# Search operations issued in batches with two buffers, last down features stacked, an end by halves, and gate weights split by halves

## The chip, the cores and the metric

The kernel runs on one core of one Trainium2 chip. The metric is the device time of one execution in microseconds, the median of several runs. The core has five engines with instruction streams of their own: TensorE (PE) for matmuls and transposes, VectorE (DVE), ScalarE (ACT), GpSimd (POOL) and SyncE (SP), which here issues DMAs. Each works its own stream in order, and they meet only in semaphores: an instruction that waits holds back all that stands behind it on its engine.

## The reference, cut to what matters

```python
# x [16, 64, 1024], ctx [16, 1601, 256], w_gate and w_up [2752, 1024], w_down [1024, 2752]
x = x + attention(layernorm(x), ctx, ctx, mask)       # 32 heads of 32 over 8 key heads
s = silu(layernorm(x) @ w_gate.T)                     # 1024 tokens x 2752 features
k = int(0.5 * 2752)
_, idx = top_k(-abs(s), k)                            # the half with the least magnitude ...
s[rows, idx] = 0.0                                    # ... becomes 0, token by token
x = x + (s * (layernorm(x) @ w_up.T)) @ w_down.T
x = x + mixture(layernorm(x))                         # 8 experts of rank 16, the top 2 by a router
```

## The kernel before, in words

All of it is one program, `fast`, in one block (L634). The 1024 tokens are 8 tiles of 128. Its stages, one after the other on TensorE, are attention (to about 594 us of the span), the gate projection, the up projection, the down projection with the mixture worked into its last third, and an end for the last two tiles. Products are made exact enough by splitting each operand in a rounded high part and a low part, and adding three products (high by high, high by low, low by high).

**Gate.** 16 passes (two halves of the tokens by 8 chunks of 352 features) of 4 tiles each make 64 slots q. For each load of weights, SP loads `g_raw`, ACT rounds it to `g_hi` in one copy (`take_weights`, L1718), POOL subtracts to `g_lo` (L1209), and the pass's first tile waits for `g_lo` (`gate`, L1981). ACT takes each slot's result from PSUM (`take_gate`), SP stores it to `s` in DRAM.

**Up.** 42 blocks i (21 chunks of 128 features by two halves of the tokens) of 24 matmuls each (`up`, L2003), into four PSUM banks: up(i) waits until ACT has copied block i - 4 (`u_copied`, L1786). POOL splits the weights (L1217, L1219). SP stores each `u_out` to `u_t`, and ACT's copy i waits for the store of i - 4.

**Search.** Beside the second half of the gate and all of up, DVE finds for each token the threshold that leaves half the features. It works in pairs of tiles, 0 to 3. `guess(p)` waits for the magnitudes of both tiles (`measure` on ACT) and gives the first cut; then come seven rounds (`search`), in which DVE counts one tile's values below the cut (L1392), ACT counts the other's (`compare`, L1746), and small DVE operations (L1399 to L1421) make the next cut. Then for each tile DVE takes the nearest values below the cut (`near`, L1429), the 8 greatest (L1435), picks the threshold, and `keep` (L1462, L1465) clears what is below it in `sx`. SP loads `mag` (three buffers) and `sx` (one buffer) from `s`, and stores the kept tile to `sk`. At which slot or block each `compare`, `measure`, load and store stands in ACT's and SP's programs is written out by hand in tables (`GATE_COUNT_AT`, `UP_COUNT_AT`, `UP_ABS_AT`, `UP_MAG_AT`, `UP_SK_AT`).

**Down.** 66 steps n: three groups of tiles (0 to 2, 3 to 5, 6 and 7) by 22 chunks of features, the last of 64. Each step turns the kept values of the group (`turn`, L2017), multiplies by `t_u` on DVE (L1495), rounds on ACT (`take_high`, L1803), subtracts on DVE (L1504), and adds 6 matmuls of 512 columns per tile to the tile's two banks (`down`, L2033). POOL splits `w_down` in three buffers (L1229, L1233) and starts a step's when the step three before it is done. The turned values come from `t_sk` blocks (two steps each, three buffers) and `t_u` chunks, loaded from ACT's queue; the first are issued at i = 40 of up. At the end the last two steps do tile 6 first, then tile 7.

**End.** For tiles 6 and 7: add to `xin` (`add_in`, L1515), layer norm (L102 to L114), turn and route (L2053, L2063), the two best experts on DVE, an exponential on ACT (L1815), `turn_hw` (L2075), `mix` (L2084), the last addition (L1561) and the store of the tile (L1070).

## Time and profile before

| | us |
|---|---|
| median of 3 runs | 1415.43 (1413.87 to 1415.97) |
| the profiled execution | 1412.86 |
| its span | 1410.9 |
| TensorE busy | 1362.0 (97%) |
| DVE busy | 981.2 (70%) |
| POOL busy | 929.2 (66%) |
| ACT busy | 739.2 (52%) |

TensorE is busy 97% of the span, so that its idle time and the length of its own work are what there is to look at. In the chain of work that ended last it has 77%, DVE 13% and DMAs 4%. The page puts the matmuls of attention (L1896, L1914, L1933), the gate (L1981), up (L2003) and down (L2033) on top. Times in the rows are us from the span's start, durations in us unless marked ns; the letter q behind an engine (SPq) marks its DMA issues.

### The profile page before, as it was taken

What the parts mean: (1) busy time and instruction counts of PE and PEld (TensorE: products, weight loads), DVE (VectorE), ACT (ScalarE), POOL (GpSimd) and SP (SyncE); (2) the same over time, 40 slices, a digit from 0 to 9 for tenths busy, and PEclk for the clock granted to TensorE, in tenths of its full rate; (3) what the DMA queues carried; (4) which work ended last, traced back from release to release, by engine and by line L of the source; (5) the groups of instructions that cost most, each with busy time, mean ns of one, the idle gap of its engine ahead of it and who ended that gap; (6) DMA issues with size and microseconds to landing.
All of it is one profiled execution on the core that took longest, in us unless ns stands there. A gap on an engine that the chain in (4) does not pass through costs nothing.

```text
span 1410.9 us, 30485 instructions
## 1 busy us (share of the span) xinstructions
PE 1362.0 (97%) x12727; PEld 1014.1 (72%) x12727; DVE 981.2 (70%) x1324; ACT 739.2 (52%) x935; POOL 929.2 (66%) x613
## 2 busy tenths in 40 slices
PE   4999999999999999899999999999997999999996
PEld 4555555555555555599999998888886888887874
DVE  6888888888888888870001899989898223255654
ACT  6788888888888888732224625243331111111211
POOL 0899888888888888813443343223233899999881
PEclk9999999999999999999999999999998999999998
DMA  9023323233333330024337348384736876855561
GB/s 357 33 104 102 136 97 114 99 117 104 117 98 121 100 107 18 16 77 169 139 124 299 122 164 276 126 294 126 275 104 244 299 258 189 272 186 181 160 202 45
DMA packets 110016, 217.62 MB, mean 154 GB/s; under 512 B 7200, under 2 KB 82864, under 8 KB 104880
## 3 DMA queue, kind: packets, MB, share of 16 engines
q1 hardware_dynamic: 88928, 192.89, 39.4%
q10 hardware_dynamic: 20944, 22.70, 5.1%
q8 instruction: 103, 1.69, 0.5%
q14 instruction: 41, 0.34, 0.1%
HBM read 173.63 MB, written 41.94 MB: 153 GB/s over the span
## 4 chain that ended last, share of the span: by engine, by line
PE 77%; DVE 13%; DMA 4%; ACT 3%; issue 2%; POOL 0%; DVEq 0%; ACTq 0%; SPq 0%
PE fast_psum L1896 16%; PE fast_psum L2033 16%; PE fast_psum L1914 15%; PE fast_psum L1981 14%; PE fast_psum L1933 6%; DVE fast_below L1392 4%; PE fast_psum L2003 2%; DMA fast_mag<-s 1%; PE fast_psum L1940 1%; PE fast_psum L2017 1%; PE fast_psum L2063 1%; DMA sk<-fast_sx 1%; PE fast_psum L2084 1%; PE fast_psum L1919 1%; DVE fast_near L1429 1%
## 5 line engine op out<-in xcount | busy, mean ns | idle before, releaser
L1322 DVE TENSOR_TENSOR fast_masked<-fast_psum,fast_mask_t 128x1024 f32<-128x1024 f32 (+1 forms) x416 | 488.2, 1218 | 72.0 <-PE fast_psum L1896 70.4
L1178 POOL TENSOR_TENSOR fast_pair<-fast_probs 128x1024 f32<-128x1024 f32 x192 | 457.0, 2383 | 96.1 <-PE fast_psum L1933 47.9
L1659 ACT ACTIVATE fast_probs<-fast_masked 128x1024 f32<-128x1024 f32 (+1 forms) x416 | 437.8, 1058 | 68.0 <-DVE fast_masked L1322 52.8
L1896 PE MATMUL fast_psum<-fast_qT,fast_kraw 32*128 32x256 f32 (+1 forms) x3328 | 245.7, 401 | 6.5 <-issue 3.3
L1914 PE MATMUL fast_psum<-fast_probs,fast_vraw 128*32 128x256 f32 (+1 forms) x3328 | 226.5, 386 | 0.8 <-ACT fast_probs L1659 0.8
L1896 PEld LDWEIGHTS fast_psum<-fast_qT,fast_kraw 32*128 32x128 f32 (+1 forms) x3328 | 152.9, 181 | 92.6 <-DVE fast_masked L1322 54.0
L1233 POOL TENSOR_TENSOR fast_d_lo<-fast_d_raw,fast_d_hi 128x256 fp32r<-128x256 f32 (+1 forms) x264 | 198.2, 781 | 5.3
L1209 POOL TENSOR_TENSOR fast_g_lo<-fast_g_raw,fast_g_hi 128x2816 fp32r<-128x2816 f32 x14 | 87.8, 6274 | 145.5 <-ACT fast_g_hi L1718 123.4
L1981 PE MATMUL fast_psum<-fast_g_hi,fast_z_hi 128*128 128x352 f32 x512 | 166.4, 325 | 1.8 <-POOL fast_g_lo L1209 1.8
L1981 PE MATMUL fast_psum<-fast_g_hi,fast_z_lo 128*128 128x352 f32 x512 | 165.5, 323 | 0.0
L1981 PE MATMUL fast_psum<-fast_g_lo,fast_z_hi 128*128 128x352 f32 x512 | 165.0, 322 | 0.0
L1914 PEld LDWEIGHTS fast_psum<-fast_probs,fast_vraw 128*32 128x32 f32 (+1 forms) x3328 | 87.1, 109 | 107.3 <-ACT fast_probs L1659 46.5
L1803 ACT CAST fast_h_hi<-fast_t_h 128x384 fp32r<-128x384 f32 (+1 forms) x66 | 31.5, 478 | 221.0 <-DVE fast_t_h L1495 206.8
L2003 PE MATMUL fast_psum<-fast_z_hi,fast_u_hi 128*128 128x512 f32 x336 | 130.8, 389 | 0.6 <-ACT fast_res L1709 0.6
L2003 PE MATMUL fast_psum<-fast_z_hi,fast_u_lo 128*128 128x512 f32 x336 | 130.7, 389 | 0.0
L2003 PE MATMUL fast_psum<-fast_z_lo,fast_u_hi 128*128 128x512 f32 x336 | 130.7, 389 | 0.0
L1495 DVE TENSOR_TENSOR fast_t_h<-fast_psum,fast_t_u 128x384 f32<-128x384 f32 (+1 forms) x63 | 32.2, 512 | 138.6 <-PE fast_psum L2017 134.7
L1217 POOL CAST fast_u_hi<-fast_u_raw 128x1024 fp32r<-128x1024 f32 x21 | 22.7, 1082 | 154.0 <-PE fast_psum L2003 90.5
L2033 PE MATMUL fast_psum<-fast_d_hi,fast_h_hi 128*128 128x512 f32 (+1 forms) x352 | 118.8, 419 | 0.7 <-issue 0.7
L1933 PE MATMUL fast_psum<-fast_pair,fast_ones 128*32 128x256 f32 x1536 | 118.1, 379 | 1.3 <-POOL fast_pair L1178 1.3
L2033 PE MATMUL fast_psum<-fast_d_lo,fast_h_hi 128*128 128x512 f32 (+1 forms) x352 | 109.9, 393 | 0.0
L2033 PE MATMUL fast_psum<-fast_d_hi,fast_h_lo 128*128 128x512 f32 (+1 forms) x352 | 109.6, 393 | 0.0
(164 smaller groups left out, 1898.2 us busy)
## 6 DMA issues: line engine op xcount, KB each, us to landing
fast_d_raw<-w_down SPq DMA_DIRECT2D x63, 512.0 KB, 3.7
fast_kraw<-ctx_t SPq DMA_DIRECT2D x32, 800.5 KB, 6.0
fast_vraw<-ctx_nat SPq DMA_DIRECT2D x16, 1536.0 KB
fast_g_raw<-w_gate_up SPq DMA_DIRECT2D x15, 1408.0 KB, 7.3
fast_mag<-s SPq DMA_DIRECT2D x8, 1376.0 KB, 9.8
fast_sx<-s SPq DMA_DIRECT2D x8, 1376.0 KB, 6.8
sk<-fast_sx SPq DMA_DIRECT2D x8, 1376.0 KB, 7.1
fast_u_raw<-w_up_t SPq DMA_DIRECT2D x21, 512.0 KB, 5.4
```

What stands on the lines that cost most here:

```text
L1178: pool.tensor_tensor(pair[:, n % PAIR_BUFS], both[:, :, 0, :], both[:, :, 1, :], ALU.add).then_inc(paired, 1)
L1209: pool.tensor_tensor(g_lo[j][:, :, :], g_raw[raw(n)][:, :, :], g_hi[j][:, :, :].bitcast(F32), ALU.subtract).then_inc(g_lo_done, 1)
L1233: last = pool.tensor_tensor(d_lo[j][0:r, qs], d_raw[j][0:r, qs], d_hi[j][0:r, qs].bitcast(F32), ALU.subtract)
L1322: dve.tensor_tensor(into, of, m, ALU.add).then_inc(mask_added, 1)
L1392: done(dve.tensor_scalar(below[0], mag[t % MAGS], cut[:, r, t:t + 1], None, ALU.is_lt, ALU.add, accum_out=count[:, t:t + 1]))
L1659: act.activation(probs[0:r, g % RING, hp * HALF:(hp + 1) * HALF], masked[0:r, h % SLOTS, :], ACT.Exp).then_inc(exp_done, 1)
L1896: last = pe.matmul(scores[0:r, (2 * g + hp) % SLOTS, h % 2, i * 256:(i + 1) * 256], kraw[b % BUFS][q, u, c * P:c * P + r], qT[q, b, u, :], ...
L1914: last = pe.matmul(o_acc[q, u, 0:256], vraw[b % BUFS][0:r, c, u * P + h * HD:u * P + (h + 1) * HD], probs[0:r, g % RING, (2 * h + i) * 256 ...
L1933: last = pe.matmul(o_acc[h * HD:(h + 1) * HD, u, 256:512], ones[:, :], pair[:, n % PAIR_BUFS, h, :], start=False, stop=final, skip_group_c ...
L1981: last = pe.matmul(bank[GATE_BANKS[q % GBANKS]][:, 0:GJ], zp[:, k, ts], wp[n % 2][:, k, :], start=(k == 0 and a == 0), stop=(k == DK - 1 a ...
L2003: last = pe.matmul(bank[i % 4][:, :], wp[f % 2][:, k, :], zp[:, k, gs], start=(k == 0 and a == 0), stop=(k == DK - 1 and a == 2))
L2033: last = pe.matmul(bank[2 * i + o][:, :], hp[jh][0:r, ts], wp[j][0:r, o * 512:(o + 1) * 512], start=(k == 0 and a == 0), stop=(k == IC - 1 ...
```

## The change

- `take_weights` rounds each gate load in two copies (4 of the 8 contraction chunks each), POOL subtracts in two, and the first tile of a pass waits for the first half at its start and for the second at its fifth chunk. The first load stays as it is.
- `sx` has two buffers and for tile 7 takes one of `mag`; its loads have a table of their own (`UP_SX_AT`), `load_mag` stands ahead of `load_sx` and `store_sk`, and the store of tile 7 stands in up's loop at f = 19.
- The comparisons of pairs 1 to 3 stand in batches of three, two and one in ACT's program, those of pair 1 behind slot 63, those of pair 2 at i = 11, 13, 16, those of pair 3 at i = 23, 25, 28. The number of rounds is the same.
- `load_block` and `load_u` of the first steps are issued at i = 34 of up; `load_block` waits for the `sk` of six tiles.
- For the last 64 features the kept values, and the weights, are loaded twice, to rows 0 to 63 and 64 to 127. POOL rounds all rows into `d_hi` and puts the low part into rows 64 to 127 of `d_hi`. So one matmul of 128 rows makes two of the three products, and one of 64 rows the third.
- Steps 63 to 65 do tile 6 first, then tile 7. In the last step each half of the columns is finished by itself (`half_done`); DVE adds it and takes its `bn_stats`. `add_out` waits for each half of `mix`, and tile 7 is stored in two halves. An exponential on a constant (`first_exp`) stands before the last use of `take_zt`.
- The slab is aligned to 128 bytes, not 512.

The diff, cut; `rows(k)` is replaced by P also in `multiply`, `take_low`, `take_high`, `turn`.

```diff
@@ -770,7 +775,8 @@
         below = [at(f"below{j}", WIDE + 3 * I + I // 2 * j, [I], BF16)[:, :] for j in range(2)]
-        sx = at("sx", WIDE + 4 * I, [I])[:, :]
+        sx_of = [at(f"sx{j}", start, [I])[:, :] for j, start in enumerate((WIDE + 4 * I, THIN + 2 * HT * GJ))]
+        sx = [sx_of[t % 2] for t in range(TILES - 1)] + [mag[(TILES - 3) % MAGS]]
         t_sk = [at(f"t_sk{j}", THIN + 3 * BW * j, [3, BW]) for j in range(2)] + [
@@ -854,6 +861,13 @@
         steps = [0]
+        g_split = lambda n, h=1: 1 if n == 0 else 2 * n + h
+        HELD = DS
+        twice = lambda n: n % IC == UF
+
+        def loads(n, ring, every=IC):
+
+            return sum(2 if m % every == every - 1 else 1 for m in range(n % ring, n + 1, ring))
...
         def u_loads(n):
...
         GATE_COUNT_AT = {42: (0, 0), 44: (0, 1), 45: (0, 2), 46: (0, 3), 48: (0, 4), 49: (0, 5)}
-        UP_ABS_AT = {6: 4, 12: 5, 19: 6, 25: 7}
-        UP_COUNT_AT = {0: (1, 0), 1: (1, 1), 2: (1, 2), 3: (1, 3), 4: (1, 4), 5: (1, 5),
-                       13: (2, 0), 14: (2, 1), 15: (2, 2), 16: (2, 3), 17: (2, 4), 18: (2, 5),
-                       26: (3, 0), 27: (3, 1), 28: (3, 2), 29: (3, 3), 30: (3, 4), 31: (3, 5)}
+        GATE_COUNTS = {63: (1, (0, 1, 2))}
+        UP_ABS_AT = {6: 4, 11: 5, 17: 6, 23: 7}
+        UP_COUNT_AT = {1: (1, (3, 4)), 4: (1, (5,)),
+                       11: (2, (0, 1, 2)), 13: (2, (3, 4)), 16: (2, (5,)),
+                       23: (3, (0, 1, 2)), 25: (3, (3, 4)), 28: (3, (5,))}
         GATE_MAG_AT = {9: 2}
-        UP_SK_AT = {1: 1, 5: 2, 7: 3, 12: 4, 13: 5, 18: 6}
-        UP_MAG_AT = {0: 4, 5: 5, 7: 6, 12: 7}
+        UP_SK_AT = {1: 1, 5: 2, 7: 3, 11: 4, 13: 5, 17: 6, 19: 7}
+        UP_SX_AT = {0: 2, 2: 3, 6: 4, 8: 5, 12: 6, 13: 7}
+        UP_MAG_AT = {0: 4, 5: 5, 7: 6, 11: 7}
         LOAD_X_AT = {0: 0, 12: 1, 30: 2}
@@ -1046,19 +1062,27 @@
             def load_sx(t):
-                if t >= 1:
-                    sp.wait_ge(sk_stored, 16 * t)
-                sp.dma_start(sx, s[t * P:(t + 1) * P, :]).then_inc(sx_full, 16)
+                if t == 1:
+                    sp.wait_ge(g_lo_done, g_split(LOADS - 1))
+                elif t == TILES - 1:
+                    sp.wait_ge(kept, t - 1)
+                elif t >= 2:
+                    sp.wait_ge(sk_stored[t % 2], 16 * (t // 2))
+                sp.dma_start(sx[t], s[t * P:(t + 1) * P, :]).then_inc(sx_full[t % 2], 16)
...
             def store_sk(t):
                 sp.wait_ge(kept, t + 1)
-                sp.dma_start(sk[t * P:(t + 1) * P, :], sx).then_inc(sk_stored, 16)
+                if t == TILES - 1:
+                    sp.wait_ge(sk_stored[t % 2], 16 * (t // 2))
+                sp.dma_start(sk[t * P:(t + 1) * P, :], sx[t]).then_inc(sk_stored[t % 2], 16)
...
             def load_down(n):
...
                 sp.dma_start(d_raw[n % DS][0:rows(k), :], w_down[k * P:k * P + rows(k), :]).then_inc(d_full[n % DS], 16)
+                if twice(n):
+                    sp.dma_start(d_raw[n % DS][UREST:P, :], w_down[UF * P:I, :]).then_inc(d_full[n % DS], 16)
@@ -1066,8 +1090,14 @@
             def store_out(t):
-                sp.wait_ge(out_added, t + 1)
-                sp.dma_start(out[t * P:(t + 1) * P, :], xin[t][:, :]).then_inc(out_stored, 16)
+                if t < TILES - 1:
+                    sp.wait_ge(out_added, 2 * t + 2)
+                    sp.dma_start(out[t * P:(t + 1) * P, :], xin[t][:, :]).then_inc(out_stored, 16)
+                    return
+                for o in range(2):
+                    os = slice(o * 512, (o + 1) * 512)
+                    sp.wait_ge(out_added, 2 * t + o + 1)
+                    sp.dma_start(out[t * P:(t + 1) * P, os], xin[t][:, os]).then_inc(out_stored, 16)
@@ -1107,9 +1137,9 @@
                 if p + 1 == PASSES:
+                    load_sx(1)
                     store_sk(0)
                     load_mag(3)
-                    load_sx(1)
                 store_gate(p)
...
                         sp.wait_ge(s_stored[j], 16 * NCH)
+                if f in UP_MAG_AT:
+                    load_mag(UP_MAG_AT[f])
+                if f in UP_SX_AT:
+                    load_sx(UP_SX_AT[f])
                 if f in UP_SK_AT:
                     store_sk(UP_SK_AT[f])
-                    if UP_SK_AT[f] + 1 < TILES:
-                        load_sx(UP_SK_AT[f] + 1)
-                if f in UP_MAG_AT:
-                    load_mag(UP_MAG_AT[f])
                 if f == UF - 2:
...
             load_down(2)
-            store_sk(TILES - 1)
             for n in range(STEPS):
@@ -1205,9 +1234,11 @@
                     pool.wait_ge(pv_done, ASTEPS)
-                pool.wait_ge(g_hi_done, n + 1)
-                pool.tensor_tensor(g_lo[j][:, :, :], g_raw[raw(n)][:, :, :], g_hi[j][:, :, :].bitcast(F32),
-                                   ALU.subtract).then_inc(g_lo_done, 1)
+                for h in range(2):
+                    ks = slice(4 * h, 4 * h + 4)
+                    pool.wait_ge(g_hi_done, g_split(n, h))
+                    pool.tensor_tensor(g_lo[j][:, ks, :], g_raw[raw(n)][:, ks, :], g_hi[j][:, ks, :].bitcast(F32),
+                                       ALU.subtract).then_inc(g_lo_done, 1)
...
             for n in range(STEPS):
-                j, r = n % DS, rows(n % IC)
-                pool.wait_ge(d_full[j], 16 * (n // DS + 1))
+                j = n % DS
+                rs, low = (slice(UREST, P), d_hi[j]) if twice(n) else (slice(0, P), d_lo[j])
+                pool.wait_ge(d_full[j], 16 * loads(n, DS))
                 if n >= DS:
...
                     pool.wait_ge(u_done, 2 * UF)
-                pool.tensor_copy(d_hi[j][0:r, :], d_raw[j][0:r, :]).then_inc(d_hi_done, 1)
+                if n % IC == 0 and n >= 1:
+                    pool.wait_ge(d_lo_done, n)
+                pool.tensor_copy(d_hi[j][:, :], d_raw[j][:, :]).then_inc(d_hi_done, 1)
                 pool.wait_ge(d_hi_done, n + 1)
...
                     qs = slice(q * 256, (q + 1) * 256)
-                    last = pool.tensor_tensor(d_lo[j][0:r, qs], d_raw[j][0:r, qs], d_hi[j][0:r, qs].bitcast(F32),
+                    last = pool.tensor_tensor(low[rs, qs], d_raw[j][rs, qs], d_hi[j][rs, qs].bitcast(F32),
                                               ALU.subtract)
@@ -1515,10 +1549,24 @@
+            def add_in_by_halves(i):
+                t = GROUPS[2][i]
+                dve.wait_ge(xin_full, 16 * TILES)
+                for o in range(2):
+                    os = slice(o * 512, (o + 1) * 512)
+                    dve.wait_ge(half_done, 2 * i + o + 1)
+                    dve.tensor_tensor(xin[t][:, os], bank[2 * i + o][:, :], xin[t][:, os], ALU.add).then_inc(added, 1)
+                    dve.wait_ge(added, 2 * t + o + 1)
+                    last = dve.bn_stats(ln3.stats[:, o, :], xin[t][:, os])
+                last.then_inc(ln3.steps_done, 1)
+
             def normalise3(t):
...
                     dve.wait_ge(z3_turned, 2 * (t - ZS + 1))
+                if t >= 6:
+                    ln3.vector_rest(dve, xin[t][:, :], z3[t % ZS][:, :], t, 1.0, z3_ready)
+                    return
                 ln3.vector(dve, xin[t][:, :], z3[t % ZS][:, :], t, 1.0, z3_ready)
@@ -1715,7 +1762,9 @@
                     act.wait_ge(g_done, n * HT)
-                act.copy(g_hi[n % 2][:, :, :], g_raw[raw(n)][:, :, :]).then_inc(g_hi_done, 1)
+                for h in range(2):
+                    ks = slice(4 * h, 4 * h + 4)
+                    act.copy(g_hi[n % 2][:, ks, :], g_raw[raw(n)][:, ks, :]).then_inc(g_hi_done, 1)
...
                     compare(*GATE_COUNT_AT[q])
+                if q in GATE_COUNTS:
+                    p, rounds = GATE_COUNTS[q]
+                    for r in rounds:
+                        compare(p, r)
...
             def load_block(q):
...
                 if b == 0:
-                    act.wait_ge(sk_stored, 16 * (GROUPS[gi][-1] + 1))
+                    stored = max(GROUPS[gi][-1] + 1, TILES - 2)
+                    for j in range(2):
+                        act.wait_ge(sk_stored[j], 16 * ((stored + 1 - j) // 2))
                 if q >= BLOCKS:
...
                               ).then_inc(sk_full[q % BLOCKS], 16)
+                if b == GB - 1:
+                    act.dma_start(t_sk[q % BLOCKS][:, 0:m, w:BW],
+                                  sk[t0 * P:(t0 + m) * P, UF * P:I].rearrange("(t p) c -> p t c", p=P)
+                                  ).then_inc(sk_full[q % BLOCKS], 16)
...
             def load_u(n):
...
                 if i in UP_COUNT_AT:
-                    compare(*UP_COUNT_AT[i])
-                if i == 2 * UF - 2:
+                    p, rounds = UP_COUNT_AT[i]
+                    for r in rounds:
+                        compare(p, r)
+                if i == 2 * UF - 8:
                     for q in range(2):
@@ -1838,6 +1900,7 @@
             ln3.scalar(act, 7)
+            act.activation(first_exp[:, :], ones[:, 0:1], ACT.Exp)
             take_zt(7)
@@ -1977,6 +2040,8 @@
                 for k in range(DK):
+                    if i == 0 and n >= 1 and k == 4:
+                        pe.wait_ge(g_lo_done, g_split(n, 1))
                     for a, (zp, wp) in enumerate(((z_hi, g_hi), (z_hi, g_lo), (z_lo, g_hi))):
@@ -2028,10 +2092,20 @@
                 ts = slice(i * P, (i + 1) * P)
-                for a, (hp, wp) in enumerate(((h_hi, d_hi), (h_hi, d_lo), (h_lo, d_hi))):
+                products = ((h_hi, d_hi, P), (h_hi, d_lo, P), (h_lo, d_hi, P))
+                if twice(n):
+                    products = ((h_hi, d_hi, P), (h_lo, d_hi, UREST))
+                if n == STEPS - 1:
+                    for o in range(2):
+                        for a, (hp, wp, r) in enumerate(products):
+                            last = pe.matmul(bank[2 * i + o][:, :], hp[jh][0:r, ts], wp[j][0:r, o * 512:(o + 1) * 512],
+                                             start=False, stop=(a == 1))
+                        last.then_inc(half_done, 1)
+                    return
+                for a, (hp, wp, r) in enumerate(products):
                     for o in range(2):
                         last = pe.matmul(bank[2 * i + o][:, :], hp[jh][0:r, ts], wp[j][0:r, o * 512:(o + 1) * 512],
-                                         start=(k == 0 and a == 0), stop=(k == IC - 1 and a == 2))
+                                         start=(k == 0 and a == 0), stop=(twice(n) and a == 1))
                 if i + 1 == len(GROUPS[gi]):
@@ -2096,7 +2170,7 @@
                 down(n, 0)
-                if n >= STEPS - 2:
+                if n >= STEPS - HELD:
                     continue
...
                     down(n, i)
-            down(STEPS - 2, 1)
-            down(STEPS - 1, 1)
+            for n in range(STEPS - HELD, STEPS):
+                down(n, 1)
             pe.wait_ge(ones_ready, 1)
```

## Rows read from the trace of the kernel before

**Rows 1.** Busy time of each engine in two stretches, granted clock, DMA share, GB/s.

```profile
851.40:1080.30 228.90, 228.79 (x1008) 189.11 (x1008) 211.54 (x341) 82.08 (x87) 65.38 (x38) 1.00 0.57 191
1080.30:1090.67 10.37, 2.42 (x10) 1.67 (x10) 6.62 (x8) 2.15 (x4) 7.91 (x10) 0.65 1.06 403
```

**Rows 2.** TensorE in order of time: start, duration, what, idle before and releaser.

```profile
1086.96 1.54 PE L2017 MATMUL fast_psum<-fast_eye,fast_t_sk 128*128 128x128 f32 x6 [6.66 <-DMA fast_t_sk<-sk]
```

**Rows 3.** The chain that ended last, start of the down stage: start, duration, what.

```profile
1090.67 5.79 PE fast_psum L2033 x18
1096.79 4.14 PE fast_psum L2033 x18
```

**Rows 4.** Columns as in rows 1, after the two stalls.

```profile
1084.00:1086.00 2.00, 0.00 (x0) 0.00 (x0) 0.91 (x4) 0.58 (x1) 1.92 (x4) 0.50 1.07 392
...
1390.00:1392.00 2.00, 2.00 (x11) 2.00 (x10) 0.83 (x2) 0.00 (x0) 0.00 (x0) 0.50 0.00 0
```

**Rows 5.** ACT in order of time: third, fifth comparison of pair 3, late copy.

```profile
1017.84 2.59 ACT L1746 ACTIVATE fast_below<-fast_mag,fast_cut 128x2752 bf16<-128x2752 f32 x1 [1.74 <-DVE fast_cut L1421]
...
1030.93 2.59 ACT L1746 ACTIVATE fast_below<-fast_mag,fast_cut 128x2752 bf16<-128x2752 f32 x1 [1.99 <-DVE fast_cut L1421]
...
1080.80 0.58 ACT L1786 COPY fast_u_out<-fast_psum 128x512 f32<-128x512 f32 x1 [10.75 <-DMA u_t<-fast_u_out]
```

**Rows 6.** DVE in order of time: cuts, rounds, `near`, pairs 1 to 3.

```profile
855.01 3.08 DVE L1462 SCALAR_TENSOR_TENSOR fast_sx<-fast_near,fast_thr,fast_sx 128x2752 f32<-128x2752 f32 x1 [0.96 <-DMA fast_sx<-s]
...
858.46 0.17 DVE L1381 TENSOR_SCALAR fast_cut<-fast_total 128x2 f32<-128x2 f32 x1
...
896.56 5.29 DVE L1429 SCALAR_TENSOR_TENSOR fast_near<-fast_mag,fast_cut 128x2752 f32<-128x2752 f32 x1
...
932.20 0.17 DVE L1381 TENSOR_SCALAR fast_cut<-fast_total 128x2 f32<-128x2 f32 x1 [3.55 <-ACT fast_mag L1740]
...
943.60 3.08 DVE L1392 TENSOR_SCALAR_CACHE_REDUCE fast_below<-fast_mag,fast_cut 128x2752 bf16<-128x2752 f32 x1
...
948.48 3.08 DVE L1392 TENSOR_SCALAR_CACHE_REDUCE fast_below<-fast_mag,fast_cut 128x2752 bf16<-128x2752 f32 x1
...
972.72 5.29 DVE L1429 SCALAR_TENSOR_TENSOR fast_near<-fast_mag,fast_cut 128x2752 f32<-128x2752 f32 x1
...
1008.07 0.17 DVE L1381 TENSOR_SCALAR fast_cut<-fast_total 128x2 f32<-128x2 f32 x1 [3.25 <-ACT fast_mag L1740]
...
1051.38 3.08 DVE L1429 SCALAR_TENSOR_TENSOR fast_near<-fast_mag,fast_cut 128x2752 f32<-128x2752 f32 x1
```

**Rows 7.** POOL and DVE in order of time, pair 0.

```profile
778.97 6.29 POOL L1209 TENSOR_TENSOR fast_g_lo<-fast_g_raw,fast_g_hi 128x2816 fp32r<-128x2816 f32 x1 [9.02 <-ACT fast_g_hi L1718]
...
781.70 3.58 DVE L1407 TENSOR_TENSOR fast_db<-fast_cut 128x2 f32<-128x2 f32 x1
```

**Rows 8.** The page's groups, part 5: first of the gate's three products.

```profile
L1981 PE MATMUL fast_psum<-fast_g_hi,fast_z_hi 128*128 128x352 f32 x512 | 166.4, 325 | 1.8 <-POOL fast_g_lo L1209 1.8
```

**Rows 9.** The same part: product of the down stage, POOL's subtraction of `w_down`.

```profile
L1233 POOL TENSOR_TENSOR fast_d_lo<-fast_d_raw,fast_d_hi 128x256 fp32r<-128x256 f32 (+1 forms) x264 | 198.2, 781 | 5.3
...
L1495 DVE TENSOR_TENSOR fast_t_h<-fast_psum,fast_t_u 128x384 f32<-128x384 f32 (+1 forms) x63 | 32.2, 512 | 138.6 <-PE fast_psum L2017 134.7
```

**Rows 10.** Groups by shape, TensorE, 1090 to 1380: 64-row matmuls.

```profile
L2033 PE MATMUL fast_psum<-fast_d_lo,fast_h_hi 64*128 64x512 f32 x12 | 3.7, 389 | 0.0
```

**Rows 11.** The end in order of time: POOL, DVE, ACT, TensorE, DVE.

```profile
1377.07 3.07 POOL L1233 TENSOR_TENSOR fast_d_lo<-fast_d_raw,fast_d_hi 64x256 fp32r<-64x256 f32 x4
...
1381.94 1.29 DVE L1515 TENSOR_TENSOR fast_xin<-fast_psum,fast_xin 128x512 f32<-128x512 f32 x2 [3.80 <-PE fast_psum L2033]
...
1395.00 1.28 ACT L1815 ACT_TABLE_LOAD   x1
...
1397.44 0.33 PE L2075 MATMUL fast_psum<-fast_eye,fast_hw 128*128 128x128 f32 x1 [0.28 <-DVE fast_hw L1549]
...
1402.60 1.41 DVE L1561 SCALAR_TENSOR_TENSOR fast_xin<-fast_psum,fast_rden,fast_xin 128x512 f32<-128x512 f32 x2 [1.04 <-PE fast_psum L2084]
```

61 lines of the change are left out of this document (32 added, 29 removed).

## The prediction

> **What bounds the kernel now.** I read the stages first, then TensorE's gaps, then what the other engines wait for where a gap is. TensorE is busy for 228.79 of the 228.90 us of the up projection, but for only 2.42 of the 10.37 us between it and the down projection [rows 1]. Up therefore ends at 1080.3. The reader is to see there that the first turn of the down stage waits 6.66 us more for `t_sk`, and that the first 18 matmuls after it take 5.79 us where the next 18 take 4.14 [rows 2, 3]: the granted clock is 0.50, the lower level of 1.2 GHz, after TensorE had stood still [rows 4]. With the clock up, the same work would have begun at 1090.67 + 1.65 = 1092.3. So the boundary costs 12.0 us. Its origin is ACT: the copy of `u_out` that stands ahead of `load_block` waited 10.75 us for a store [rows 5], since SP stood at `store_sk(6)` and its load.
>
> Behind up, another chain runs: the search on DVE. A pair's first cut comes at 858.46, 932.20 and 1008.07, and the first `near` of the pair 38.1, 40.5 and 43.3 us later [rows 6]. Two of these starts waited for `mag` (3.55 and 3.25 us) [rows 6]. DVE also stands behind POOL: L1407, a 128x2 operation, took 3.58 us and ended when POOL's 6.29 us subtraction did (785.28 and 785.26) [rows 7]. The gate loses 1.8 us in all to `g_lo` [rows 8]. In the rest of the down stage TensorE is full, and after it comes a serial tail.
>
> **The sum is made on the profiled execution**, 1412.86 us (span 1410.9 and 2.0 around it). The median of the runs shown is 1415.43, 2.6 above it. I subtract from the median what I find in the trace.
>
> **Gate by halves.** The first half of `g_lo` is there after half a cast and half a subtraction, about 4.4 us earlier; the second half is wanted half a tile (1.9 us) later than all of it is now. Both old gaps together are 1.8 us [rows 8] and each is shorter than that: I take -1.8. Two more instructions per load on ACT and POOL lie beside TensorE. The 14 new waits in the middle of a tile I take at 0: 64 tiles start behind satisfied waits, and all gaps of that line are the 1.8 us [rows 8]; the other bound is 0.06 each, 0.8. POOL is also done 1.2 us sooner per load, and three small DVE operations of pair 0 end with POOL [rows 7]: about 3.6 us for the search.
> The Trainium skill, page "SBUF — State Buffer", section "SBUF: two separate sides", says that GpSimd and a DVE operation with two SBUF inputs take one port pair as an exclusive lock, first come first served. The rows on L1407 agree. By that rule a 3 us DVE operation could also slip in between the two halves and hold the second back by 3.1 us; against 1.9 us of cover that is at most 1.2 us at each of three late loads, which would give back the 1.8.
>
> **Search, its loads, and what ACT now waits for.** SP loads `mag` ahead of the `sk` store, and `sx` has two buffers. This takes the two waits for `mag` (6.8 us) and one of 0.96 for `sx` off DVE [rows 6]. Pair 0 ends at 858.46 - 3.6 - 1.0 = 854. From there a pair takes its search (I take 40 us of the 38.1 to 43.3) and its two tiles: 1008.07 - 3.25 - 972.72 = 32.1. So pair 2 starts at 854 + 72.1 = 926.1, pair 3 at 998.2.
> Here the change adds the wait that decides. `compare(p, 0), (p, 1), (p, 2)` stand one after the other in ACT's program, at i = 11 and i = 23, and the first waits for the pair's first cut. Behind them stand the copies of `u_out`; up(i) waits for copy i - 4. The up stage without holds runs from 851.5 - 1.8 = 849.7 in 42 blocks of 5.446 us. In pair 3 the third comparison ended about 12.4 us after the first cut (two rounds, clear of POOL) and the fifth started 22.9 us after it and took 2.6 [rows 5, 6]. With the copy this makes 13.0 and 26.1 us.
> Up(16) is free at 936.8, but copy 12 comes at 926.1 + 13.0 = 939.1: held 2.3 us. Up(18) cannot start before 952.2, two blocks after up(16) are 950.0: 2.2 more. Up(28) would start at 849.7 + 152.5 + 4.5 = 1006.7 and copy 24 comes at 1011.2: 4.5 more. Up(30): 1024.3 against 1022.1, 2.2 more. The holds sum to 11.2, and up ends at 1078.5 + 11.2 = 1089.7. The lower bound is no hold at all: rounds clear of POOL are 4.88 us [rows 6], 35.6 for a search, so pair 3 starts at 989 or earlier. The upper is a pair like the slowest, 43.3 + 32.8, after a pair 0 that gained only the 0.96: pair 3 at 1009.7, holds of 22.7. In pair 1 the batch stands after slot 63: copy 0 comes at 867, up(4) is free at 871.5; no hold.
> The one gap of over 4 us may cost clock. The first stall of rows 2 had the clock at 0.50 by 1084, so it fell within 3.7 us of the last matmul; after it, it cost 1.65 us. I take 0.5 here, since up(30) is held anyway; bounds 0 and 3.4. Up ends at 1090.2.
>
> **Boundary.** `t_sk` and `t_u` are now loaded at i = 34 (about 1045), when six tiles of `sk` are stored, and the search is over by 1072. What is left is turn, product, rounding and subtraction, four steps of about half a us each (the product is 0.51 [rows 9]): 2.1. The down stage starts at 1092.3, against 1092.3. The boundary's gain and the gate's are spent on the holds: 0.
>
> **Stacked last features.** A 64-row matmul takes 0.389 us, as long as those of 128 rows [rows 10] whose 18 take 4.14, 0.23 each [rows 3]. Per tile six become four. In the first two groups 6 tiles x 2 x 0.23 = -2.75. Nothing is waiting there: POOL's step is one cast and four subtractions of 0.78 [rows 9], 4.2 us against 4.5 on TensorE, with three buffers. Three more DMAs on SP and on ACT's queue stand in front of loads that are three steps ahead.
>
> **End.** With HELD = 3 TensorE has two tiles' worth (2.75 us) to do before step 65, where it had 4.1. POOL begins that step's `d` only when step 62 is done, and its last subtraction ends at 1380.14 [rows 11]; TensorE will idle 1.4 us for it, and the first half of tile 6 is there at 1380.95. The two additions and the two `bn_stats` (2.62 us) then start 1.0 us earlier than at 1381.94 [rows 11], less 0.1 for the added wait: -0.9. Tile 7's matmuls (3.7 us) end as before, beside DVE. `first_exp` takes the table load of 1.28 us [rows 11] from the path, but route(7) ends only 0.28 us before `turn_hw(6)` [rows 11]: -0.28. The last addition by halves leaves one of two operations (1.41 us) after the last matmul: -0.7. The last store of 256 KB in place of 512: at the 392 GB/s of rows 4 it is -0.65; less a second issue I take -0.5. The slab's finer alignment and the wait for `ones` add no work: 0. Together -2.4 (bounds -1.0 and -3.3; with the clock staying up at the end, where it fell to 0.50 [rows 4], 2.6 more).
>
> Sum: 0 - 2.75 - 2.4 = -5.15. On the profiled execution 1407.7, on the median 1410.3; I say **1410**.
>
> **Rivals.**
> 1. The batches don't hold TensorE. For: the copies have three blocks (16.3 us) of cover, and the search was blocked for only 2 us in pair 1. Then up ends at 1078.5, down starts at 1080.6, and the boundary gives 11.7: 1398.5. Against: with every pair at its fastest observed, 38.1, pair 3 still starts at 994 and holds about 7 us are left. Partial holds lie between. Chance 0.20.
> 2. Slower: the search stays as slow as pair 3 was, since each small DVE operation that meets POOL waits up to 2.4 us, and ACT, waiting in its batch, passes this on to TensorE. Holds 22.7, up ends 1101.7, down starts 1103.8: +11.5 - 5.15, so 1421.8. It decides from a third pair that starts after 1003; up to there the result is no loss. Chance 0.13.
> 3. The change does not do what it says at the end and in the gate: TensorE waits for step 65, the clock is down, the halves are blocked by DVE. Then only the stacking is left, partly eaten by cold blocks in up: -1, 1414.5. Chance 0.15.
> Forecast: holds of 8 to 15 us, 1406 to 1414; chance 0.52.
>
> The Trainium skill, "TensorE: Matmul & The Clock Gate", section "HAM oscillation — how this bites in real kernels", warns that each gap between bursts of matmuls can put the clock down anew. The clock at 0.50 after both old gaps [rows 4] agrees. By it each of the four new holds could cost what the old one did, four times 1.65, which belongs to rival 2.
>
> **Numbers.** A measurement here tells a change from none at about 0.2%, 2.8 us. Faster by more: all of rival 1 and 0.38 of the forecast, 0.58. Within: 0.14 of the forecast and 0.11 of rival 3, 0.25. Slower: rival 2 and 0.04 of rival 3, 0.17. Range 1401 to 1418: it leaves out half of rival 1 and most of rival 2; the forecast's own is 1406 to 1414.
>
> **What would show it.** Gaps of TensorE in front of up(16), (18), (28), (30) of 2 to 5 us, each ended by a copy of `u_out`; no gap on `g_lo`; the first cuts at 854, 926 and 998; down's first matmul 2.1 us after up's last; step 65 waiting 1.4 us for `d_lo`. No gaps in up would prove rival 1; a third first cut after 1003, rival 2.

## The result and the profile after

The changed kernel takes 1420.43 us (median of 6 runs, 1418.94 to 1424.91); the kernel before, on the same chip, 1414.42 (1413.87 to 1415.97). The ratio is 1.004, 95% interval 1.0023 to 1.0058. It is slower by 6.0 us; the forecast was 1410, and 1420.4 lies above its range of 1401 to 1418. Rival 2 had named the place and 1421.8.

The profiled run took 1418.94 us, span 1417.0 against 1410.9.

| in the traces, us | before | after |
|---|---|---|
| attention's last block starts | 590.66 | 592.68 |
| up starts, counted from there | 260.85 | 259.03 |
| gaps of TensorE in up, behind its first matmul | none over 0.1 | 11.36 and 5.21 |
| up ends, first turn of down starts | 1080.3, 1086.96 | 1102.2, 1102.01 (they overlap) |
| first matmul of down | 1090.67, at the lower clock (1092.3 if warm) | 1104.34, warm |
| from there to the end of the span | 318.6 | 312.7 |

I call a hold a wait of TensorE in front of a block of up: up(i) may not start before ACT has copied block i - 4. The next rows are TensorE in order of time (start, duration, what, idle before and who ended it): both holds, the matmuls behind the first, and the start of down. They answer to [rows 2, 3].

```profile
950.40 0.77 PE L2068 MATMUL fast_psum<-fast_z_hi,fast_u_hi 128*128 128x512 f32 x1 [11.36 <-ACT fast_u_out L1845]
950.96 0.63 PE L2068 MATMUL fast_psum<-fast_z_lo,fast_u_hi 128*128 128x512 f32 x1
951.39 0.63 PE L2068 MATMUL fast_psum<-fast_z_hi,fast_u_lo 128*128 128x512 f32 x1
...
1023.87 0.77 PE L2068 MATMUL fast_psum<-fast_z_hi,fast_u_hi 128*128 128x512 f32 x1 [5.21 <-ACT fast_u_out L1845]
...
1102.01 0.82 PE L2082 MATMUL fast_psum<-fast_eye,fast_t_sk 128*128 128x128 f32 x6
1103.24 0.52 PE L2082 MATMUL fast_psum<-fast_eye,fast_t_sk 128*128 128x128 f32 x3 [0.41 <-DVE fast_t_h L1529]
1104.34 0.70 PE L2107 MATMUL fast_psum<-fast_d_hi,fast_h_hi 128*128 128x512 f32 x2 [0.57 <-issue]
```

The boundary's wait of 6.66 us is gone as forecast. But the matmuls behind a hold start every 0.43 us and not every 0.23: the clock had fallen. The windows of the two holds (columns as in rows 1) show a mean granted clock of 0.72 and 0.69, and still 0.97 in the stretch between them. From 951 to 955 it is 0.50, the lower level. The three windows:

```profile
935.00:952.00 17.00, 5.64 (x22) 4.36 (x21) 16.06 (x37) 9.01 (x9) 3.05 (x2) 0.72 0.06 21
952.00:1018.00 66.00, 66.00 (x284) 54.41 (x283) 64.05 (x88) 23.57 (x23) 25.52 (x12) 0.97 0.65 219
1018.00:1026.00 8.00, 2.79 (x8) 1.99 (x8) 7.38 (x27) 4.55 (x7) 0.00 (x0) 0.69 0.18 65
```

ACT in order of time, where the first hold comes from: the batch at i = 11 waits 9.72 us for the pair's first cut, and only behind its third comparison come copies 12 and 13, for which up(16) and up(17) wait.

```profile
938.19 2.59 ACT L1795 ACTIVATE fast_below<-fast_mag,fast_cut 128x2752 bf16<-128x2752 f32 x1 [9.72 <-DVE fast_cut L1415]
...
947.10 2.59 ACT L1795 ACTIVATE fast_below<-fast_mag,fast_cut 128x2752 bf16<-128x2752 f32 x1 [2.21 <-DVE fast_cut L1455]
949.60 0.19 ACT L1795 ACTIVATION_READ_ACCUMULATOR fast_below<-fast_mag,fast_cut 128x1 f32 x1
949.69 1.05 ACT L1845 COPY fast_u_out<-fast_psum 128x512 f32<-128x512 f32 x2
```

And DVE, answering to [rows 6]: the first cuts of pairs 1, 2, 3, and operations between them that are several times as long as their size asks for.

```profile
858.68 0.17 DVE L1415 TENSOR_SCALAR fast_cut<-fast_total 128x2 f32<-128x2 f32 x1 [1.64 <-ACT fast_mag L1789]
...
877.82 2.37 DVE L1451 TENSOR_TENSOR fast_db<-fast_off 128x2 f32<-128x2 f32 x1
...
907.72 2.35 DVE L1478 TENSOR_TENSOR fast_goes<-fast_hit,fast_top 128x8 f32<-128x8 f32 x1
...
918.57 5.24 DVE L1463 SCALAR_TENSOR_TENSOR fast_near<-fast_mag,fast_cut 128x2752 f32<-128x2752 f32 x1
...
935.85 2.31 DVE L1415 TENSOR_SCALAR fast_cut<-fast_total 128x2 f32<-128x2 f32 x1
...
1009.31 2.31 DVE L1415 TENSOR_SCALAR fast_cut<-fast_total 128x2 f32<-128x2 f32 x1
```

POOL beside the first of them. The 128x2 operation at 877.82 ends when POOL's subtraction ends (880.19 and 880.17):

```profile
876.66 1.04 POOL L1248 CAST fast_u_hi<-fast_u_raw 128x1024 fp32r<-128x1024 f32 x1 [10.11 <-DMA fast_u_raw<-w_up_t]
877.78 2.39 POOL L1250 TENSOR_TENSOR fast_u_lo<-fast_u_raw,fast_u_hi 128x1024 fp32r<-128x1024 f32 x1
```

A pair takes 77.2 us (935.85 - 858.68) and 73.5 (1009.31 - 935.85). In the kernel before it took 73.7 and 75.9, but with waits of 3.55 and 3.25 us for `mag` in them: 70.2 and 72.6 of work. The waits went, and pair 1 took 7 us more in exchange. None of it is DVE waiting for ACT: the operations themselves are longer.

### The profile page after: what moved, and what is told of

Read it like the earlier page. It is cut to its first block, busy times and chain, and to the rows that moved or that the text cites. A ratio compares the mean times of both kernels' runs of the same rounds, so it can differ in the third digit from the quotient of the medians.

```text
span 1417.0 us, 30491 instructions
## 1 busy us (share of the span) xinstructions
PE 1361.3 (96%) x12711; PEld 1010.5 (71%) x12711; DVE 984.5 (69%) x1324; ACT 741.1 (52%) x950; POOL 943.1 (67%) x627
## 3 DMA queue, kind: packets, MB, share of 16 engines
q8 instruction: 101, 1.65, 0.5%
## 4 chain that ended last, share of the span: by engine, by line
PE 81%; DVE 14%; ACT 2%; issue 1%; DMA 1%; SPq 0%; POOL 0%; POOLq 0%; ACTq 0%; DVEq 0%
PE fast_psum L1959 16%; PE fast_psum L2046 16%; PE fast_psum L2107 15%; PE fast_psum L1977 15%; PE fast_psum L1996 6%; PE fast_psum L2068 6%; DVE fast_below L1426 4%; PE fast_psum L2003 1%; PE fast_psum L2082 1%; DVE fast_near L1463 1%; DMA fast_mag<-s 1%; PE fast_psum L2158 1%; PE fast_psum L1982 1%; PE fast_psum L2137 1%; DVE fast_sx L1496 1%
## 5 line engine op out<-in xcount | busy, mean ns | idle before, releaser
L1356 DVE TENSOR_TENSOR fast_masked<-fast_psum,fast_mask_t 128x1024 f32<-128x1024 f32 (+1 forms) x416 | 488.3, 1218 | 74.0 <-PE fast_psum L1959 72.1
L1267 POOL TENSOR_TENSOR fast_d_lo<-fast_d_raw,fast_d_hi 128x256 fp32r<-128x256 f32 x252 | 189.4, 781 | 5.0
L1240 POOL TENSOR_TENSOR fast_g_lo<-fast_g_raw,fast_g_hi 128x1408 fp32r<-128x1408 f32 x28 | 90.0, 3238 | 140.4 <-ACT fast_g_hi L1767 118.3
L2068 PE MATMUL fast_psum<-fast_z_hi,fast_u_hi 128*128 128x512 f32 x336 | 133.0, 396 | 17.2 <-ACT fast_u_out L1845 16.6
L1248 POOL CAST fast_u_hi<-fast_u_raw 128x1024 fp32r<-128x1024 f32 x21 | 34.4, 1638 | 165.3 <-DMA fast_u_raw<-w_up_t 101.1
L2107 PE MATMUL fast_psum<-fast_d_hi,fast_h_hi 128*128 128x512 f32 x348 | 116.6, 416 | 0.6 <-issue 0.6
L2107 PE MATMUL fast_psum<-fast_d_lo,fast_h_hi 128*128 128x512 f32 x336 | 104.2, 391 | 0.0
```

The costliest lines, as they stand in the source:

```text
L1240: pool.tensor_tensor(g_lo[j][:, ks, :], g_raw[raw(n)][:, ks, :], g_hi[j][:, ks, :].bitcast(F32), ALU.subtract).then_inc(g_lo_done, 1)
L1267: last = pool.tensor_tensor(low[rs, qs], d_raw[j][rs, qs], d_hi[j][rs, qs].bitcast(F32), ALU.subtract)
L1356: dve.tensor_tensor(into, of, m, ALU.add).then_inc(mask_added, 1)
L2068: last = pe.matmul(bank[i % 4][:, :], wp[f % 2][:, k, :], zp[:, k, gs], start=(k == 0 and a == 0), stop=(k == DK - 1 and a == 2))
L2107: last = pe.matmul(bank[2 * i + o][:, :], hp[jh][0:r, ts], wp[j][0:r, o * 512:(o + 1) * 512], start=(k == 0 and a == 0), stop=(twice(n) an ...
```

## The experiments

Ratios are against the kernel before, run beside each (1413.9 to 1414.6 us), with 95% intervals. Waits are given with the tile that TensorE waited for: `u_out` is ACT's copy, `u_lo` the weights that POOL splits. A search is the time from a pair's first cut to its first `near`.

| kernel | us | ratio | pairs 1, 2: first cut to first cut | waits of TensorE in up |
|---|---|---|---|---|
| the change | 1420.4 | 1.004 [1.002, 1.006] | 77.2, 73.5 | 11.4, 5.2 on u_out |
| spread | 1409.7 | 0.996 [0.994, 0.997] | 71.1, 75.1 | 2.0, 2.2 on u_lo |
| batches in before | 1434.1 | 1.014 [1.012, 1.015] | 74.0, 81.4 | 5.9, 11.7 on u_out, 1.2 on u_lo |
| quarters | 1409.6 | 0.998 [0.996, 0.999] | 71.8, 70.6 | 4.5, 2.6 on u_out |
| batches later | 1418.3 | 1.003 [1.001, 1.004] | 77.0, 74.5 | 7.3, 6.1, 1.9, 0.8 on u_lo |
| spread, SP eased | 1404.5 | 0.992 [0.990, 0.994] | 76.4, 78.0 | 1.3 on u_out, 0.4 to 1.2 three times on u_lo |
| spread, SP eased, quarters | **1399.3** | 0.989 [0.988, 0.991] | 73.2, 71.7 | none |
| spread, quarters | 1402.0 | 0.991 [0.988, 0.993] | 69.5, 74.3 | 1.3, 4.2 on u_lo |
| batches, SP eased, quarters | 1412.0 | 0.998 [0.997, 0.999] | 73.3, 70.9 | 3.7, 3.7 on u_out |
| tail alone | 1412.7 | 0.998 [0.997, 0.999] | 75.1, 76.7 | 1.5 on u_lo |
| gate alone | 1415.0 | 1.000 [0.999, 1.001] | 74.8, 75.4 | none |
| loads alone | 1414.3 | 0.999 [0.998, 1.001] | 71.2, 75.2 | 2.1, 8.0 on u_lo |
| quarters in before | 1408.9 | 0.996 [0.995, 0.997] | 71.8, 74.8 | none |

**Spread: one comparison per block.**

```diff
-        GATE_COUNTS = {63: (1, (0, 1, 2))}
+        GATE_COUNTS = {}
...
-        UP_COUNT_AT = {1: (1, (3, 4)), 4: (1, (5,)),
-                       11: (2, (0, 1, 2)), 13: (2, (3, 4)), 16: (2, (5,)),
-                       23: (3, (0, 1, 2)), 25: (3, (3, 4)), 28: (3, (5,))}
+        UP_COUNT_AT = {0: (1, (0,)), 1: (1, (1,)), 2: (1, (2,)), 3: (1, (3,)), 4: (1, (4,)), 5: (1, (5,)),
+                       13: (2, (0,)), 14: (2, (1,)), 15: (2, (2,)), 16: (2, (3,)), 17: (2, (4,)), 18: (2, (5,)),
+                       26: (3, (0,)), 27: (3, (1,)), 28: (3, (2,)), 29: (3, (3,)), 30: (3, (4,)), 31: (3, (5,))}
```

> The changed kernel with one comparison of ACT per block of up again (pair 1 at i = 0 to 5, pair 2 at 13 to 18, pair 3 at 26 to 31, none at the gate's end); all other parts stay. Theory A, the batches: TensorE was held 11.4 and 5.2 us for copies of u_out that stood behind a batch, and the rounds of the search, no longer in step with up's blocks of 5.44 us, ran into POOL's casts and subtractions, which made a pair's way from first cut to near 41.8 us where it was 38.1. So here both holds go, first cut to near falls back to 38 to 39 us, down's first matmul comes at about 1084 in place of 1104.3, and the time is 1400 (1397 to 1403). Theory B, the search was slow for another reason (its loads, the second buffer of sx, the start 2 us later): cuts of pairs 2 and 3 stay at about 936 and 1009, holds of several us remain in front of up(17) and later, time 1412 to 1420.

Both holds went and the kernel gained 10.8 us, so theory B fell. But the time missed theory A's 1400 by 10, and half of theory A fell with it: the searches of pairs 1 to 3 did not become shorter (38.9, 42.6 and 40.8 us for 41.8, 38.9 and 38.0). In pair 2, 4.1 of the 42.6 us are waits of DVE for ACT's comparisons, which now stand one per block. And TensorE met a wait that theory A did not have, for `d_lo` (2.12 us, at the start of down) and for `u_lo`:

```profile
1005.95 0.50 PE L2066 MATMUL fast_psum<-fast_z_hi,fast_u_hi 128*128 128x512 f32 x1 [2.00 <-POOL fast_u_lo L1248]
...
1073.71 0.50 PE L2066 MATMUL fast_psum<-fast_z_hi,fast_u_hi 128*128 128x512 f32 x1 [2.15 <-POOL fast_u_lo L1248]
```

**The batches alone, in the kernel before** (the change's three tables and the loops that read them).

> The kernel before with nothing but the new tables of ACT's batches (three comparisons after slot 63 and two at i = 1, then 3, 2, 1 at i = 11, 13, 16 and 23, 25, 28). Theory A: the batches alone hold TensorE in front of up(16) by about 10 us and up(28) by about 13, and slow each search by 3 to 4 us; since 12 us of the old boundary wait then lie beside the holds, the time rises by 11 to 15 us only, 1426 to 1429. Theory B (the batches are harmless, the new order of loads and stores in SP is what held the search): 1413 to 1416, first cut to near 38 to 43 us as before, no gap over 1 us in up.

Theory A's direction, but 19.7 us where 11 to 15 were expected; the clock after the holds and 3.7 us of waits for `d_lo` in down were not in it. The holds came, but the searches were not slowed: 38.5, 38.4 and 36.0 us, where the kernel before has 38.1, 40.5 and 43.3. Pair 2 takes 81.4 us because `keep` waits 7.05 us for `sx`. So what the batches do is to hold ACT's queue; they do not by themselves make a search long. By themselves they cost more than the whole change does.

**Batches three blocks later.**

```diff
-                       11: (2, (0, 1, 2)), 13: (2, (3, 4)), 16: (2, (5,)),
-                       23: (3, (0, 1, 2)), 25: (3, (3, 4)), 28: (3, (5,))}
+                       14: (2, (0, 1, 2)), 16: (2, (3, 4)), 18: (2, (5,)),
+                       26: (3, (0, 1, 2)), 28: (3, (3, 4)), 30: (3, (5,))}
```

> The changed kernel with the batches of pairs 2 and 3 three blocks later (i = 14, 16, 18 and 26, 28, 30), pair 1 as it is. Theory A: the copy behind a batch now comes at about 949 and 1021, when up(19) and up(31) are free at 955 and 1020.5, so no hold is longer than 1 us although the search stays as slow (41 to 42 us from first cut to near); down starts at about 1084, time 1400 to 1403. Theory B, the batch's place is not what held TensorE: a hold of 5 us or more moves to another block, 1412 or more.

Theory A missed by 15 us or more. ACT's holds went as it said, but waits of 7.3 and 6.1 us for `u_lo` took their place, and pairs 2 and 3 searched for 44.1 and 45.9 us where 41 to 42 were expected. SP's queue in order of time shows why: `load_up` at 1074.88 stands behind `store_sk(6)`, for which SP had waited 22.2 us.

```profile
1048.66 0.55 SPq L1050 DMA_DIRECT2D fast_u_raw<-w_up_t  x1
1071.47 0.32 SPq L1077 DMA_DIRECT2D sk<-fast_sx  x1
1071.83 3.00 SPq L1056 DMA_DIRECT2D u_t<-fast_u_out  x2
1074.88 1.12 SPq L1050 DMA_DIRECT2D fast_u_raw<-w_up_t  x1
```

The change had put this store at f = 17, which without holds comes at 1037, and tile 6 was kept at 1071.5. In the changed kernel nothing was seen of it (SP waited only 2.2 us at that store), because TensorE was already late. So the theory became: the search is late, and whichever queue waits for it first, ACT's or SP's, hands that on to TensorE.

**Quarters: POOL's subtraction for up in four pieces.**

```diff
-                pool.tensor_tensor(u_lo[j][:, :, :], u_raw[j][:, :, :], u_hi[j][:, :, :].bitcast(F32),
-                                   ALU.subtract).then_inc(u_lo_done, 1)
+                for h in range(4):
+                    hs = slice(2 * h, 2 * h + 2)
+                    last = pool.tensor_tensor(u_lo[j][:, hs, :], u_raw[j][:, hs, :], u_hi[j][:, hs, :].bitcast(F32),
+                                              ALU.subtract)
+                last.then_inc(u_lo_done, 1)
```

> The changed kernel with POOL's subtraction for up (2.40 us) as four quarters of 0.6 us, so that a DVE operation that waits behind POOL gets in sooner. If POOL is what slows the search (theory A): the DVE operations of 0.15 us that take 2.4 us now (two or three per pair) take 0.6 to 0.8, the near of 5.24 us takes about 3.7, a pair falls from 77.2 and 73.4 us to about 71 and 69, the third pair starts at about 1000, the holds sink from 16.6 to 5 to 9 us, time 1409 to 1413. If the search is not slowed by POOL's subtraction, or only by its cast (theory B), pairs and holds stay, 1418 to 1421. A third way: operations of 3.1 us of DVE slip between the quarters and make u_lo late, then gaps of TensorE on u_lo appear.

Near theory A in all points: the `near` that took 5.2 us takes 3.5 to 3.6, pairs 71.8 and 70.6, holds 7.0 together, 1409.6.

**Spread, and SP's table later, with and without quarters.**

```diff
-        UP_SK_AT = {1: 1, 5: 2, 7: 3, 11: 4, 13: 5, 17: 6, 19: 7}
-        UP_SX_AT = {0: 2, 2: 3, 6: 4, 8: 5, 12: 6, 13: 7}
-        UP_MAG_AT = {0: 4, 5: 5, 7: 6, 11: 7}
+        UP_SK_AT = {1: 1, 6: 2, 8: 3, 13: 4, 14: 5, 19: 6, 20: 7}
+        UP_SX_AT = {0: 2, 2: 3, 7: 4, 9: 5, 14: 6, 15: 7}
+        UP_MAG_AT = {0: 4, 6: 5, 8: 6, 12: 7}
```

> The changed kernel with three edits: one comparison of ACT per block (as in the spread kernel), SP's stores of sk, loads of sx and of mag put one or two tiles of up later (sk at f = 1, 6, 8, 13, 14, 19, 20), and POOL's subtraction for up in quarters. Theory A+: two queues passed the late search on to TensorE, ACT's (copies of u_out behind comparisons) and SP's (loads of w_up behind store_sk, seen as waits of 2.0 and 2.15 us for u_lo in the spread kernel and 7.3 and 6.1 in the one with later batches). With both out of the way and the search 3 to 4 us per pair faster, no gap over 1 us in up, down's first matmul at 1082 to 1083, and 312.7 us from there to the end as in the changed kernel: span 1395 to 1397, time 1397 to 1400. If the start happens to be 2 us later, 1401. Rival: the search itself is the limit, DVE comes late to the first turns, and the time stays at 1404 or more.

> The same without the quarters: the spread kernel with only SP's positions moved. Theory A+ (SP's queue cost the spread kernel its 2.0, 2.15 and 2.12 us): these three waits go, down's first matmul comes at 1082 to 1084 in place of 1088.6, time 1399 to 1404 against 1409.7. Rival (the waits of u_lo come from the DMA queue or from POOL behind DVE's operations): they stay, time 1407 to 1411.

The first came in as worked out for up, with down's first matmul at 1082.69; from there to the end it took 315.0 us where 312.7 were expected, since the clock fell once more in down (last section). TensorE waits in up and at the boundary for nothing longer than 0.6 us; this is all that the view of waits lists for it between 851 and 1105 us:

```profile
PE fast_psum L2069 <- ACT fast_res L1757: 0.6, 1, 0.6
PE fast_psum L2108 <- issue: 0.6, 1, 0.6
PE fast_psum L2083 <- DVE fast_t_h L1530: 0.4, 1, 0.4
```

Against the change its trace gives the price of the two holds directly. Up starts at 851.75 here and at 851.71 there; the first turn comes at 1080.37 and at 1102.01. Of these 21.6 us, 16.6 are the holds, 5.1 are blocks at the lower clock.

POOL in the same trace shows what the quarters do: a long operation of DVE slips in between them, four of them take 8.45 us where 2.8 are usual. TensorE did not wait for it.

```profile
983.87 8.45 POOL L1250 TENSOR_TENSOR fast_u_lo<-fast_u_raw,fast_u_hi 128x256 fp32r<-128x256 f32 x4
...
994.75 2.83 POOL L1250 TENSOR_TENSOR fast_u_lo<-fast_u_raw,fast_u_hi 128x256 fp32r<-128x256 f32 x4
```

Without quarters the median is 1404.5, just above theory A+'s 1399 to 1404, and the waits for `u_lo` are 1.2 us at most where they were 2.2, so the rival fell. But the four runs lie between 1401.5 and 1411.1, where with quarters they lie within 1.6 us. The profiled one is the slowest: pair 3's search takes 47.4 us in it, and down's second turn waits 7.4 us for a product of DVE, which is still searching. DVE's rows say why: one small operation after the other meets POOL.

```profile
1023.48 2.36 DVE L1451 SCALAR_TENSOR_TENSOR fast_da<-fast_db,fast_da 128x2 f32<-128x2 f32 x1
...
1035.85 2.33 DVE L1449 TENSOR_TENSOR fast_db<-fast_off 128x2 f32<-128x2 f32 x1
...
1047.45 2.37 DVE L1442 SCALAR_TENSOR_TENSOR fast_da<-fast_da 128x2 f32<-128x2 f32 x1
```

**Spread and quarters without SP's table.**

> The spread kernel with POOL's subtraction for up in quarters, SP's positions unmoved: the fourth corner beside 1409.7 (spread), 1404.5 (spread, SP eased) and 1399.3 (all three). Theory A+: what holds TensorE is the lateness of the search against the tables, so a faster search makes SP's positions matter less: waits for u_lo of 0 to 1.5 us in all, 1400 to 1403. Rival (the positions of SP matter by themselves: store_sk(6) at f = 17 stands 15 us too early whatever the search does): the waits of 2 us stay, 1404 to 1407.

The median, 1402.0, is in theory A+'s range, but in the profiled run (1404.5, the four lie between 1399.2 and 1404.9) the waits for `u_lo` are 1.3 and 4.2 us, where theory A+ had 1.5 at most; that is the rival's reading. So SP's positions seem to matter by themselves, by some 3 us; the intervals, 0.988 to 0.993 and 0.988 to 0.991, overlap, so that this rests on the one trace.

**The batches put back into the fastest kernel.**

> The fastest kernel so far (1399.3: spread, SP eased, POOL in quarters) with the change's batches of comparisons put back. Theory A: with SP and POOL out of the way the batches hold TensorE as in the kernel with quarters alone, where the two holds were 4.5 and 2.6 us and the time 1409.6; a third comparison 13 to 14 us after first cuts at about 930 and 1001 against up(16) and up(28) free at 938 and 1003 plus the first hold gives 5 to 7 and 2 to 6 us, and 2 to 3 us for the clock after a stall: 1406 to 1412. Rival (the batches were harmful only while the search was slow or SP late): holds under 2 us in all, 1399 to 1402.

Two holds of 3.7 us, 1412.0: the rival fell. With POOL and SP out of the way the batches still cost 12.7 us, holds, clock and all.

**The parts of the change alone.** Each is the kernel before with one part of the change's diff.

> The kernel before with only the stacked last features and the end (three tiles held, halves of the last tile, first_exp, the last addition and store by halves; the slab's alignment of 128 comes with it). Prediction's terms: -2.75 and -2.4 us, so 5.15 less than before, 1409 beside 1414.3; the boundary's waits and the search stay as they were. In the changed kernel the stretch from down's start to the end was 5.9 shorter, by which 1408.4. Rival (the terms are eaten up by the step that waits for d_hi, or by the clock): less than 3 us of difference. The start of the attention stage tells on the side whether the alignment moves it: 590.7 if it doesn't and the 2 us were chance, 592.7 if it does.

> The kernel before with only the gate by halves (casts, subtractions and TensorE's waits). Prediction's term: up starts 1.8 us earlier, no gap on g_lo, pair 0 of the search ends 3 to 4 us earlier. Since the down stage waits for the last sk store and the search behind it, the gain at the end is what the search gains: pair 1's first cut moves only if mag is there. Theory A: 0 to -3 us, 1411 to 1414. Rival (three instructions more per load disturb ACT or DVE): 1415 or more.

> The kernel before with only the second buffer of sx, SP's new order and the loads of t_sk and t_u at i = 34; one comparison of ACT per block. By difference (spread kernel 1409.7, tail alone 1412.7, gate alone 1415.0) this part should be worth -3 to -5 us: 1409 to 1412. Its own mechanism: no wait of 3.3 us or more for mag in front of the first cuts of pairs 2 and 3, no wait of 6.7 us for t_sk, against it 2 us waits for u_lo behind SP's stores. Rival (the waits for u_lo take back all of it): 1414 or more.

Tail: only 1.7 us, and the expectation of 5.15 missed. Its trace has the gain and what ate it: from down's first matmul to the end 316.6 us against 320.3, with a clock fallen after a stall of 1.87 us in it (below); and ahead of down the pairs of the search took 1.3 and 0.9 us longer, and up waited 1.5 us for `u_lo`. Gate: no gap on `g_lo`, up starts 2.1 us sooner counted from attention's last block, and the time doesn't change; the first turn of down still waits 6.57 us for `t_sk`. Loads: my difference of the others said -3 to -5 and was wrong, the rival right: the waits for `mag` and `t_sk` are gone, and SP's early stores (26.0 us of waiting at the longest) give waits of 2.1 and 8.0 us for `u_lo` in exchange. The three parts alone add up to -1.4 us where together, in the spread kernel, they gave -4.6: their prices do not add, since each moves what the others meet.

**Quarters in the kernel before.**

> The kernel before with only POOL's subtraction for up in quarters. Theory A (the search bounds the boundary between up and down, and POOL's subtraction slows the search): the near of 5.29 us take about 3.6, pair 3's rounds lose their waits of 2.4, the last tile but one of sk is kept 4 to 7 us sooner (at about 1063 in place of 1068.7), the wait for t_sk sinks from 6.7 to 1 to 3 us, down starts 4 to 6 us earlier: 1408 to 1411. Rival (in step with up's blocks the search hardly meets POOL, so quarters give nothing here): 1413.5 to 1415.5.

5.7 us gained, as theory A said, without any part of the change. In its trace down's first matmul comes at 1083.54, 7.1 us sooner, with no wait left for `t_sk`; a wait of 2.06 us for `d_lo` some 20 us into down takes part of that back.

## Why the prediction was wrong

**The step that failed** is "From there a pair takes its search (I take 40 us of the 38.1 to 43.3) and its two tiles: 1008.07 - 3.25 - 972.72 = 32.1", and with it "pair 2 starts at 926.1, pair 3 at 998.2". What the runs show in its place: a pair has no fixed length, it grows with each DVE operation that falls on one of POOL's. Less the 2.0 us by which this trace runs later, they started at 933.9 and 1007.3. The 9.1 us of pair 3 come from three places:
- Pair 0: 3.4 us gained where 4.6 were taken, and then a wait of 1.64 us for `mag` that I had not seen. Pair 1's first cut came at 856.7 for 854: 2.7.
- Pair 1: 77.2 us for 72.1, so 5.1. The search took 41.8 and the two tiles 35.4.
- Pair 2: 73.5 for 72.1, so 1.4. Its search took 38.9, less than I had taken; its tiles 34.6.

The 32.1 is the same in pairs 1 and 2 of the kernel before, but it is no constant: in each of them three operations between `near` and the next cut met POOL and lost 3.5 us, in pair 1 of the changed kernel five did and lost 6.6 (`near` 2.2, L1478 2.2, three of 0.7 to 0.9). The quarters show the cause, with pairs 5.3 and 2.8 us shorter in the changed kernel. I had written this down as rival 2's mechanism, with 1003 as the point from which it decides, and gave it 0.13; 38.1 to 43.3 in three pairs should have told me that a pair's length is a matter of how it lies to POOL, and that every shift deals it anew.

**The holds** follow from these starts by the prediction's own arithmetic, but not all of them: up(16) is free at 936.8 and copy 12 at 933.9 + 13.0 = 946.9 gives 10.1, measured 11.36; for up(28) it gives 5.8, measured 5.21. The holds of 2.2 us in front of up(18) and up(30) never came. The fifth comparison ended 24.4 us after the first cut in both pairs, where 25.5 were taken, and the two blocks behind each long hold were themselves late by the clock: up(18) started at 964.1, more than 3 us after its copy. Together 16.6 us of holds, for 11.2 forecast and 20.3 by that arithmetic. The 32.8 us in the prediction's upper bound stand in no row; the rows give 32.1 twice.

**The clock** is the second wrong term: 0.5 us taken, with 3.4 as the upper bound, 5.1 measured, in two holds. The Trainium skill, page "TensorE: Matmul & The Clock Gate", section "HAM oscillation — how this bites in real kernels", warns of a new fall with each gap; the trace agrees, both holds were followed by matmuls at the lower level (granted clock 0.50 from 951 to 955 and from 1023 to 1027). The text priced that at four times 1.65 = 6.6 and then counted it only to rival 2. That rival's 1421.8 comes close to the 1420.4 partly by luck: it had 22.7 us of holds, the trace has 16.6, and the clock fills the rest.

**What was right.** The gate: -1.8 by the table above, no gap left. The wait of 6.66 for `t_sk` is gone, and from down's first turn to its first matmul it takes 2.3 us where 2.1 was worked out. That the loads at i = 34 did this the changed kernel does not show, since TensorE came so late there: the batches alone, with the loads unmoved, have no such wait either. The profiled run with SP eased shows it: its first turn, at 1082.64, does not wait, though DVE works on pair 3 until 1089. The end: -3.9 for -2.4; half of it is clock, an upside that stood in the bounds with 2.6. The kernel before had routed tile 6 at the lower level (granted clock 0.50 from 1388 to 1394), the changed one did not (1.00 from 1396 to 1402); first the row before, then those after:

```profile
1388.79 3.99 PE L2063 MATMUL fast_psum<-fast_aw,fast_zt 128*128 128x136 f32 x16 [0.68 <-ACT fast_zt L1810]
```

```profile
1390.31 0.50 PE L2101 MATMUL fast_psum<-fast_d_hi,fast_h_hi 128*128 128x512 f32 x1 [1.12 <-POOL fast_d_hi L1267]
...
1398.28 2.12 PE L2137 MATMUL fast_psum<-fast_aw,fast_zt 128*128 128x136 f32 x16 [0.73 <-ACT fast_zt L1871]
```

Step 65 waited for POOL's `d_hi` as said, 1.1 us for 1.4.

**Stacking** came out near its price, but only in part by its reason. Down's first two groups take 194.9 us for 196.9 (from 1092.3, the start if warm), so -2.0 where -2.75 was taken. The price had every matmul at 0.23 us. In the stacked step those of 128 and of 64 rows alternate by twos and start every 0.33 us at a granted clock of 1.00:

```profile
1197.72 0.71 PE L2107 MATMUL fast_psum<-fast_d_hi,fast_h_hi 128*128 128x512 f32 x2
1198.36 0.73 PE L2107 MATMUL fast_psum<-fast_d_hi,fast_h_lo 64*128 64x512 f32 x2
1199.02 0.74 PE L2107 MATMUL fast_psum<-fast_d_hi,fast_h_hi 128*128 128x512 f32 x2
```

Four take 1.32 us where six took 1.38; from the step's first matmul to the next group's the gain is 0.37 us per group. In step 65, where they alternate one by one, they start every 0.43 us (from 1390.31 on), so that four take longer than the six did. The other 1.2 us of the -2.0 lie in the steps before the last, 4.45 us each for 4.47, and in a shorter start of the last step; why is open.

**The sum.** Forecast for the span 1410.9 - 5.15 = 1405.8, measured 1417.0, 11.2 more. Holds and clock give 21.7 for 11.7, so +10.0; stacking and end together -5.9 for -5.15, so -0.8; the late start of the trace +2.0. That start is not the change's by any evidence: attention's last block begins between 590.5 and 592.7 in the profiles of these fourteen kernels, whose code up to there is the same or differs only in the slab's alignment, and both alignments show early and late ones (592.3 with 512, 590.5 with 128). What sets it stays open.

**What stays open.** Why the search of a given kernel falls into or out of POOL's way is not shown. What is shown is the spread: in pairs 1 to 3 of the nine profiles without quarters a search took 36.0 to 47.4 us, 41.3 in the mean, in the five with them 36.0 to 42.8, 39.4 in the mean. That one comparison per block keeps the rounds in step with up's blocks of 5.44 us and with POOL's 10.88, as I wrote before the first experiment, held in pair 1 (38.9 us) but not in pairs 2 and 3 (42.6 and 40.8). It is no general remedy, and in pair 2 it costs the 4.1 us of waits for ACT.

## What to carry over

When a step off the critical path grows nearly as long as the stage that covers it, every queue that waits for it in program order is a way on to the path: ask for each engine and for SP what stands behind the wait, and price them all, since removing one only shows the next. Don't make a due time from one favourable sample where another engine's lock can add several us per round; cut the locking operation into pieces first, and then move loads and comparisons. Here the pieces gained in each of the four kernels that differ by nothing else: 5.7 us in the kernel before, 10.8 in the changed one, 7.6 in the spread one, 5.2 with SP eased. Whether they also make a kernel's runs more alike is not shown: they did with SP eased, but in the kernel before the ten runs with quarters lie 6.7 us apart. The kernel that comes out of it, one comparison per block, POOL's subtraction in quarters and SP's table one to two tiles later, takes 1399.3 us, 15.2 less than the kernel before and 21.2 less than the change.

## What the runs showed of the hardware

- A small DVE operation that meets POOL's subtraction lasts until that ends (880.19 and 880.17 above): those of 128x2 take up to 2.38 us beside POOL's 2.40 and at most 1.04 where POOL works in quarters; `near` takes up to 5.29 and, with quarters, 3.45 to 3.92. It is not only those with two inputs, as I had it: the first cut, a TENSOR_SCALAR with one tensor and 128x2, took 2.31. DVE's comparisons of 128x2752 (L1426) took 3.08 us in every kernel, whatever POOL did. The Trainium skill, page "SBUF — State Buffer", section "SBUF: two separate sides", says that the lock is exclusive, goes to whoever starts first, and is wanted by DVE's faster two-port modes as well as by two inputs; the rows agree, and POOL loses by it too: four quarters took 8.45 us.
- The same stall does not always cost the same. TensorE waits 1.8 to 1.9 us for `zt` between 1290 and 1324 us in every kernel. In ten of the fourteen profiles it goes on at full speed, 14.9 us from there to the next such wait; in four (spread, tail alone, the fastest kernel and the one with its batches put back) the clock falls (granted 0.57 from 1290 to 1292 in the fastest kernel) and the stretch takes 16.5 to 17.2. The row is the fastest kernel's; in the kernel before its 16 matmuls take 2.12 us. I found no rule in which kernels it happens.

```profile
1289.59 3.38 PE L2138 MATMUL fast_psum<-fast_aw,fast_zt 128*128 128x136 f32 x16 [1.87 <-ACT fast_zt L1872]
```

- Matmuls of 512 columns that alternate between 128 and 64 rows start every 0.33 us when they alternate by twos and every 0.43 one by one, where those of one height, 128 or 64 rows, start every 0.23, all at a granted clock of 1.00 (down's last steps above and in the kernel before).
